# One ScalarE eviction and three VectorE additions per unit in the last stage, instead of two and two with a GpSimd addition

## The reference, cut to what matters

```python
def _L1_ffn_ref(x, gate_up_packed, gate_up_scales, down_packed, down_scales):
    I = gate_up_packed.shape[0] // 2                                   # 1408
    w_gu = _dequant_fp4(gate_up_packed, gate_up_scales, GROUP_SIZE)    # codes * scale of (group of 128 inputs, output)
    w_down = _dequant_fp4(down_packed, down_scales, GROUP_SIZE)
    gate_up = jnp.einsum('bsh,oh->bso', x, w_gu)
    gate, up = (gate_up[..., :I], gate_up[..., I:])
    h = jax.nn.silu(gate) * up
    y = jnp.einsum('bsi,hi->bsh', h, w_down)
    rms = jnp.sqrt(jnp.mean(y * y, axis=-1, keepdims=True) + EPS)
    return y / rms
...
x = x + _L1_ffn_ref(_layernorm(x, axis=-1), ...)
```

## Time and profile before

| | us |
|---|---|
| median of three runs | 1701.52 |
| the profiled execution's own time | 1699.38 |
| its span (first to last instruction of the core) | 1697.6 |
| PE, DVE, ACT, POOL busy over the span | 1475.3, 1368.7, 922.5, 660.9 |
| last stage, batch 0 begins (first unit) | at 1347.77 |
| last stage, batch 1, batch 3 begin | at 1443.67, 1610.94 |
| L2019, VectorE addition | 176 of 748 ns |
| L1905, ScalarE eviction | 88 + 88 of 685 and 687 ns |
| L1785, GpSimd addition | 88 of 1445 ns |

### The profile page before, as it was taken

One profiled execution on the slowest core, in us unless ns is written; L12 is line 12 of the kernel. 1 busy time (PEld: TensorE's weight loads), 2 busy tenths in 40 slices (PEclk: granted clock), 3 DMA queues, 4 the chain that ended last, 5 costly groups with the idle time before them and its releaser, 6 DMA issues. The chain is left out here.

```text
span 1697.6 us, 20354 instructions
## 1 busy us (share of the span) xinstructions
PE 1475.3 (87%) x6524; PEld 609.1 (36%) x6524; DVE 1368.7 (81%) x2017; ACT 922.5 (54%) x1221; POOL 660.9 (39%) x442
## 2 busy tenths in 40 slices
PE   5898998997654896889989998999899888999998
PEld 1332433432213432433344334334433333343433
DVE  6999989999999875799867976897688599656554
ACT  3766666565335200457665765576467543646464
POOL 2999999999971514100010010000000233333343
PEclk8899998998897998879999999999999999999999
DMA  8455555456549973410001000000100400000000
GB/s 253 117 146 150 138 155 146 142 146 158 151 112 238 222 137 119 186 47 2 1 1 47 2 1 18 18 1 1 35 1 1 103 1 0 26 1 25 1 25 25
DMA packets 65255, 131.50 MB, mean 77 GB/s; under 512 B 11376, under 2 KB 11376, under 8 KB 64384
## 3 DMA queue, kind: packets, MB, share of 16 engines
q1 hardware_dynamic: 53104, 104.07, 21.7%
q0 software_dynamic: 7168, 25.17, 6.4%
q10 hardware_dynamic: 4880, 0.95, 0.3%
HBM read 134.11 MB, written 12.85 MB: 87 GB/s over the span
## 5 line engine op out<-in xcount | busy, mean ns | idle before, releaser
L1611 DVE TENSOR_REDUCE att_mx<-att_ring 128x1 f32<-128x512 f32 x512 | 322.4, 684 | 40.6 <-PE att_ring L1219 35.1
L372 POOL TENSOR_TENSOR ssm_dBu<-ssm_du,ssm_BC 128x1024 f32<-128x1024 f32 x128 | 304.4, 2384 | 17.4 <-DVE ssm_du L408 17.4
L1436 ACT ACTIVATE att_Pr<-att_psT 128x1024 f32<-128x1024 f32 x256 | 249.1, 1023 | 87.1 <-PE att_psT L1245 83.6
L267 PE MATMUL ssm_psY<-ssm_hC,ident 128*128 128x512 f32 x512 | 253.7, 626 | 38.1 <-POOL ssm_hC L379 20.6
L336 ACT ACTIVATE ssm_dA<-ssm_delta,ssm_negA 128x512 f32<-128x512 f32 x256 | 165.3, 682 | 165.5 <-DVE ssm_hC L428 164.1
L1785 POOL TENSOR_TENSOR mlp_both<-mlp_first,mlp_third 128x512 f32<-128x512 f32 x88 | 127.1, 1445 | 225.2 <-DVE mlp_first L2019 114.1
L2019 DVE SCALAR_TENSOR_TENSOR mlp_first<-mlp_psQ,mlp_s_gu,mlp_first 128x512 f32<-128x512 f32 x176 | 131.6, 748 | 99.7 <-ACT mlp_first L1905 89.6
L473 DVE TENSOR_TENSOR_SCAN ssm_dA<-ssm_dA,ssm_dBu 128x512 f32<-128x512 f32 x148 | 178.7, 1220 | 17.0 <-ACT ssm_dA L336 13.7
L1219 PE MATMUL att_ring<-att_KT,att_QT 64*128 64x512 f16 x512 | 168.3, 392 | 11.4 <-DVE att_mx L1611 4.0
L267 PEld LDWEIGHTS ssm_psY<-ssm_hC,ident 128*128 128x128 f32 x512 | 95.1, 196 | 187.7 <-issue 91.4
L1835 PE MATMUL mlp_psD<-mlp_Wd,mlp_hT 128*128 128x512 f32 x352 | 158.2, 595 | 0.4 <-DVE mlp_Wd L1988 0.4
(11 more groups left out here) (276 smaller groups left out, 2286.1 us busy)
## 6 DMA issues: line engine op xcount, KB each, us to landing
ssm_BC<-bc_rows SPq DMA_DIRECT2D x128, 512.0 KB, 4.9
moe_W<-in_masksT POOLq DMA_DIRECT2D x32, 512.0 KB, 9.4
late_words<-in_gate_upT SPq DMA_DIRECT2D x32, 176.0 KB, 3.9
X<-in_x SPq DMA_DIRECT2D x4, 1024.0 KB, 11.0
rows<-moe_XP SPq DMA_DIRECT2D x4, 1024.0 KB, 14.0
out_x<-X SPq DMA_DIRECT2D x3, 1024.0 KB, 4.2
mlp_Wd<-in_downT SPq DMA_DIRECT2D x8, 352.0 KB, 9.6
ssm_ctxP<-in_ctxT SPq DMA_DIRECT2D x4, 512.0 KB, 12.5
```

The lines of the kernel that those rows point to most:

```text
L267: nc.tensor.matmul(psY[:, w, :], ident[:], hC[:, w, g % RC, :], start=False, stop=(n == DS - 1)).then_inc(summed, 1)
L372: nc.gpsimd.tensor_tensor(dBu[:, g % RB], du[:, b % 2, hh * W:(hh + 1) * W, :], BC[:, g % RING, 0, :].unsqueeze(1).broadcast_to([P, W, S]) ...
L1436: nc.scalar.activation(Pr[:, i % NP_], psT[:, i % 2], ACT.Exp).then_inc(exp_done, 1)
L1611: nc.vector.tensor_reduce(mx[:, m % 3, qt, row_order(j)], bank(("score", i)), AX.X, ALU.max).then_inc(maxed, 1)
```

## The change

`third` and `both` are dropped, and with them GpSimd's loop and its semaphore. ScalarE evicts group 0 alone, into `total`, which has two buffers by the parity of the block. VectorE adds groups 1, 2 and 3 to it in place, each waiting for the one before. The silu and `gated` read `total` and wait for VectorE's count. TensorE waits for ScalarE before group 0 and for VectorE before groups 1, 2 and 3.

```diff
+    ADDS = DT - 1
-        first = sb("first", [P, 2, S])
-        third = sb("third", [P, 2, S])
-        both = sb("both", [P, 2, S])
+        total = sb("total", [P, 2, 2, S])
...
-                for U in range(B * UNITS):
-                    J, w = divmod(U, 2)
-                    pool.wait_ge(ev_a, 2 * U + 2)
-                    pool.wait_ge(ev_v, 2 * U + 2)
-                    if J >= 1:
-                        pool.wait_ge(h_done if w else silu_done, J)
-                    nc.gpsimd.tensor_tensor(both[:, w, :], first[:, w, :], third[:, w, :], ALU.add).then_inc(summed, 1)
...
                 def turn(b):
                     if b >= 1:
-                        pe.wait_ge(ev_a, 2 * UNITS * b)
-                        pe.wait_ge(ev_v, 2 * UNITS * b)
+                        pe.wait_ge(ev_a, UNITS * b)
+                        pe.wait_ge(ev_v, ADDS * UNITS * b)
...
                         elif u >= 1:
-                            pe.wait_ge(ev_v if g % 2 else ev_a, 2 * (U - 1) + g // 2 + 1)
+                            pe.wait_ge(ev_v if g else ev_a, ADDS * (U - 1) + g if g else U)
...
-                        for g, dst in ((0, first), (2, third)):
-                            act.wait_ge(grp, DT * U + g + 1)
-                            if g == 0 and U >= 2:
-                                act.wait_ge(summed, U - 1)
-                            nc.scalar.activation(dst[:, w, :], psQ[:, g, :], ACT.Copy, scale=s_gu[:, row, g:g + 1]).then_inc(ev_a, 1)
+                        act.wait_ge(grp, DT * U + 1)
+                        if J >= 2:
+                            act.wait_ge(h_done if w else silu_done, J - 1)
+                        nc.scalar.activation(total[:, J % 2, w, :], psQ[:, 0, :], ACT.Copy, scale=s_gu[:, row, 0:1]).then_inc(ev_a, 1)
...
                         if w == 1:
-                            act.wait_ge(summed, 2 * J + 1)
+                            act.wait_ge(ev_v, ADDS * (2 * J + 1))
                             if J >= 2:
                                 act.wait_ge(h_done, J - 1)
-                            nc.scalar.activation(sg[:, J % 2, :], both[:, 0, :], ACT.Silu).then_inc(silu_done, 1)
+                            nc.scalar.activation(sg[:, J % 2, :], total[:, J % 2, 0, :], ACT.Silu).then_inc(silu_done, 1)
...
                 def gated(J):
                     dve.wait_ge(silu_done, J + 1)
-                    dve.wait_ge(summed, 2 * J + 2)
+                    dve.wait_ge(ev_v, ADDS * (2 * J + 2))
                     if J >= HT:
                         dve.wait_ge(down, J - HT + 1)
-                    nc.vector.tensor_tensor(hT[:, J % HT, :], sg[:, J % 2, :], both[:, 1, :], ALU.mult).then_inc(h_done, 1)
+                    nc.vector.tensor_tensor(hT[:, J % HT, :], sg[:, J % 2, :], total[:, J % 2, 1, :], ALU.mult).then_inc(h_done, 1)
...
-                        for n, g in enumerate((1, 3)):
+                        y = total[:, (b * JT + j) % 2, w, :]
+                        for g in range(1, DT):
                             dve.wait_ge(grp, DT * U + g + 1)
-                            if n == 0:
-                                dve.wait_ge(ev_a, 2 * U + 1)
+                            if g == 1:
+                                dve.wait_ge(ev_a, U + 1)
                             else:
-                                dve.wait_ge(ev_v, 2 * U + 1)
-                            nc.vector.scalar_tensor_tensor(out=first[:, w, :], in0=psQ[:, g, :], scalar=s_gu[:, row, g:g + 1], in1=first[:, w, :],
+                                dve.wait_ge(ev_v, ADDS * U + g - 1)
+                            nc.vector.scalar_tensor_tensor(out=y, in0=psQ[:, g, :], scalar=s_gu[:, row, g:g + 1], in1=y,
                                                            op0=ALU.mult, op1=ALU.add).then_inc(ev_v, 1)
```

More of the change, by code:

```diff
@@ L1754, in stage_mlp @@
         xn_done, turned, xh_done, xl_done = (sem(n) for n in ("xn_done", "turned", "xh_done", "xl_done"))
-        grp, ev_a, ev_v, summed, silu_done, h_done, down, wd_done = (
-            sem(n) for n in ("grp", "ev_a", "ev_v", "summed", "silu_done", "h_done", "down", "wd_done"))
+        grp, ev_a, ev_v, silu_done, h_done, down, wd_done = (
+            sem(n) for n in ("grp", "ev_a", "ev_v", "silu_done", "h_done", "down", "wd_done"))
         squared, eps_done, root2, inverted, added, last_rows = (sem(n) for n in (
```

## The result

The changed kernel takes 1725.46 us in the median (1724.77 to 1727.79), beside 1700.85 for the kernel before on the same chip: ratio 1.0149 with an interval of 1.0127 to 1.0170, 24.6 us slower. Its profiled execution took 1724.85 us with a span of 1723.0.

The account below looks back on a forecast made before the run. TensorE was taken to bound batches 1 to 3, VectorE batch 0. Steady periods 19.5, starts 5.6 and batch 0 0.7 made 25.8 us on 1699.38, 1725.2; with 2.1 for the median, 1727, range 1717 to 1736.

Parts of the forecast that it names:

- Steady periods, 19.5 us: Batches 1 to 3: TensorE waits for a third chained addition, each of 24 periods grows 0.81 us, from 6.97 to 7.78.
- VectorE's room, silu, statistics and normalisation at nothing: Steady periods: VectorE is done 5.4 us into 7.78, so statistics, normalisation and the later silu cost nothing.
- Starts, 5.6 us: Starts of batches 1 to 3: replayed chains put the first down product 1.9 us later per start, 5.6 in all.
- Batch 0, +0.7 us: Batch 0: two more VectorE additions per block, 1.70 us, against relief from GpSimd; sum +0.7, bounds -3 and +17.
- -0.3 for blocks 0 to 2: Start of batch 0: first block's gain and a little back from the low-clock stretch, -0.3 us, bounds -2 and +2.
- The rule of the exclusive port lock: Batch 0: VectorE and GpSimd lock a shared port pair, so relief without GpSimd is whole and batch 0 costs +0.7.
- The rival of the clock: Batch starts: TensorE's clock may fall to 1.2 GHz, costing 3 to 10 us in all, 1730 to 1737; chance 0.18.
- No relief: Batch 0: the long decoding instructions are not GpSimd's doing, so batch 0 costs 17 us, 1743; chance 0.04.
- additions held up by GpSimd: VectorE's 748 ns additions shorten to 0.43 us or less without GpSimd, no steady stall, 1685 to 1700; chance 0.04.

Follow-up runs that it names:

- e2: Changed kernel, but in the w = 0 units ScalarE evicts group 2 too and VectorE's third addition reads it from SBUF: 1704.60 us, ratio 1.0029.
- e3: Changed kernel, but in the w = 1 units ScalarE evicts group 2 too and VectorE's third addition reads it from SBUF: 1729.55 us, ratio 1.0182.
- e5: Changed kernel with two of a down product's four row blocks moved between the w = 0 and the w = 1 unit: 1705.03 us, ratio 1.0025.
- e8: Kernel before, with five idle matmuls on TensorE ahead of each of units 2 to 5 of batch 0: 1700.23 us, ratio 0.9994.
- e1: Changed kernel with GpSimd adding an idle tile to itself behind each unit, as load alone: 1737.21 us, ratio 1.0218.
- e4: Kernel before with GpSimd's addition alone dropped: ScalarE evicts groups 0 and 2 as before, VectorE adds the third sum itself: 1706.95 us, ratio 1.0037.

## Why the prediction was right, step by step

The forecast was 1727 us, the median is 1725.46; on the profiled executions the sum said +25.8 and the spans differ by 25.4. Some of that closeness is luck. Terms were off in both directions, the stage itself grew by 24.3, and the 1.1 us that bring it to 25.4 came from stages that the change doesn't touch.

- *Steady periods, 19.5 us.* Right in place and size: 20.4. The period was put at 7.78 and is 7.82. The chained pitch is 0.855 rather than 0.85, which gives 0.01. Besides, the prediction had the second addition of before just touch TensorE, and it didn't: in the period of the earlier trace rows group 3 starts 0.43 behind group 2, TensorE's own pace. e2 against e3 shows that the w = 0 unit alone carries it, e5 that it goes when the additions stay and cover comes. Both were only argued before.
- *VectorE's room, silu, statistics and normalisation at nothing.* Right: the starts and the one block of 8.17 apart, the steady blocks of batches 1 and 2 are as long as batch 3's, which has no statistics.
- *Starts, 5.6 us.* Too much by 1.2: 4.4. The replay put ScalarE's silu and third eviction too late by 0.8 us, since I set its instructions end to end at their full record lengths, while in the trace one starts up to 0.1 ahead of the end of the one before. VectorE's nine additions of units 0 to 2 run on without a wait (7.20 us from 1629.56 in batch 3), so they, not ScalarE, pace unit 2, and everything behind it comes 0.4 earlier than replayed.
- *Batch 0, +0.7 us.* Wrong in sign, by 1.5: -0.77. Every block from 3 to 9 is within about 0.05 of its working (8.91 and 8.90 for the blocks with statistics, 7.80 for block 9). What was mis-sized is the "-0.3 for blocks 0 to 2", and in two ways. It is less than the prediction's own list gives for two of them, 0.4 for the first block and 0.2 for block 1, and both came true on VectorE (4.76 for 5.19 and 7.58 for 7.78); with them the list adds up to +0.4 before any clock. And the stretch with the low clock was taken to stay nearly as it was, and it went: the changed kernel's granted clock is 1.00 over the whole of batch 0, and block 2 takes 7.81 on VectorE instead of 8.93. e8 prices that at 1.2 us. Beside e8, where the clock stays up too, the changed kernel's batch 0 is 0.4 us longer (95.13 and 94.74), which is what the list says.
- *The rule of the exclusive port lock* gave a batch 0 near zero against +17, and e1 bears it out: with an addition of idle data on GpSimd the decoding is long again. The Trainium skill ("SBUF — State Buffer", Who interferes with whom) calls the port pair that VectorE and GpSimd share an exclusive lock. The traces agree: the long instructions end a fixed 0.28 or 0.55 us behind GpSimd's addition.
- *The rival of the clock* came true as a mechanism and not as a price. The windows of the changed kernel's starts of batches 1 and 2, and TensorE's timeline of batch 1:

```profile
1457.00:1461.00 4.00, 3.59 (x9) 0.81 (x10) 3.79 (x7) 0.83 (x2) 0.00 (x0) 0.59 0.39 152
1548.00:1553.00 5.00, 4.36 (x12) 0.81 (x10) 4.69 (x8) 0.69 (x1) 0.00 (x0) 0.66 0.28 106
```

```profile
1455.48 0.39 PE L1814 MATMUL mlp_psQ<-mlp_xh,late_Vgu 128*128 128x512 f16 x1 [1.75 <-DVE mlp_total L2011]
...
1457.19 0.61 PE L1814 MATMUL mlp_psQ<-mlp_xh,late_Vgu 128*128 128x512 f16 x1 [0.25 <-DVE mlp_total L2011]
...
1460.36 0.38 PE L1815 MATMUL mlp_psQ<-mlp_xl,late_Vgu 128*128 128x512 f16 x1
1460.88 0.39 PE L1814 MATMUL mlp_psQ<-mlp_xh,late_Vgu 128*128 128x512 f16 x1
```

In all three starts the clock went to the lower level of 1.2 GHz behind a stall of 1.75 us between groups 0 and 1 of unit 4. It was back, about 3 us later, before the first down product. The groups in between are paced by the additions at 0.85, which is also what a group takes at 1.2 GHz (its two records start 0.43 apart there). It cost nothing, and e1 is the control: it has the same starts, 20.75, 20.72 and 20.72, and its clock stayed full in those of batches 1 and 2, as its windows show:

```profile
1470.00:1480.00 10.00, 6.07 (x22) 1.93 (x22) 9.45 (x16) 3.57 (x5) 3.87 (x3) 1.00 0.28 105
1562.00:1572.00 10.00, 6.07 (x22) 1.75 (x21) 9.48 (x15) 3.77 (x5) 3.70 (x3) 1.00 0.28 104
```

e5 moves half a down product into that stretch and pays 2.2 to 2.7 us in two of three starts; in e3 a whole one fell into it once. What decides whether and when the clock falls is open. The prediction argued from the length of one stall, and that is not enough. The fall of batch 0 vanished where the longest stall there had gone from 2.08 to 1.14, but e4 has stalls of 1.93 at unit 4 of all four batches and a full clock in all of them, and behind the same 1.75 e1 and e3 kept theirs in some batches and not in others.
- *No relief, and additions held up by GpSimd*: both fell. The additions are 749 ns with GpSimd idle.

## What to carry to other kernels

When a reader of a PSUM bank is moved from an engine that works beside another to the end of a chain on that other, count not the load of the engine but the time from the first read to the last, and lay it against the writer's time until it comes back to that bank; here 2.5 us stood against 1.7. The same work is nearly free again when something that needs none of those banks is put between: e5 won 22.3 us in the steady periods by a change of order alone, and 20.4 between the medians. And read what an engine off the critical path does to its neighbours: GpSimd's addition was cheap where VectorE had room and cost it up to 1.9 us per block in batch 0, where VectorE was the bound. Against that stand the two sums per block that VectorE does in its place, so the net was small: 0.8 us for batch 0 in e4. In the other batches the same move cost 1.6 us per start. So the choice is worth making batch by batch.

## What was not expected of the hardware

- TensorE's clock fell at three batch starts for about 3 us each and the time didn't move, since a group of matmuls at the lower level takes as long as the VectorE addition that it waited for (0.85 us). With a down product in the stretch a fall cost 1.6 us (e3) to 2.7 us (e5). It stayed down for about 3 us in one start of e5 and for about 7 in the other two, behind stalls of equal length.
- A VectorE instruction that met a GpSimd addition ended a fixed 0.28 or 0.55 us behind it, whether the two ran together for a third of a microsecond or for more than one.
- The stages before the last, the same code in all, began the last stage anywhere from 1347.8 to 1354.4 us. An effect of 1 or 2 us is read from its own stretch, not from a total.
